# Graph block, last part: the results' stores move from the sync engine's queue to GpSimd's own queue

## The reference

```
x = layernorm(x + attention(x, adj))            # 16 heads, adj added twice as bias
top1   = argmax(mean(x over nodes) @ router_w + router_b)        # one of 4 experts per graph
out    = adj @ (x @ expert_w[top1])
mean, var = moments of out over all graphs of one expert
y      = relu((out - mean) * rsqrt(var + eps) * gamma[top1] + beta[top1])
result = layernorm(x + y)                       # over the 512 features of each node
```

## Time and profile before

| | |
|---|---|
| median of 3 runs | 2736.3 us (2734.73 to 2736.76) |
| the profiled execution's own time | 2736.11 us |
| its span | 2734.3 us |
| last part, from its first DMA issue | from 2483.2 us of the span |
| POOL in the whole span | 885.3 us busy |
| DMA in the whole span | mean 198 GB/s |

### The profile page before, as it was taken

The page is one execution under the profiler, slowest core; times in us unless marked ns, Lnnn a source line. Parts: engine busy times, 40 slices in busy tenths (PEclk is TensorE's granted clock), DMA queues, the critical chain, the costliest instruction groups (busy, mean ns, idle before and its releaser), DMA issues. The chain is left out here.

```text
span 2734.3 us, 61236 instructions
## 1 busy us (share of the span) xinstructions
PE 2580.7 (94%) x20250; PEld 2139.9 (78%) x20250; DVE 2111.7 (77%) x4097; ACT 1783.6 (65%) x6186; POOL 885.3 (32%) x489
## 2 busy tenths in 40 slices
PE   7999999999999999999999999999999999965665
PEld 6788888888888888888888888888888888754554
DVE  5977877877777778778777777777787777864887
ACT  4666666666666666666666666666666666645987
POOL 1132332323323333323223233333232232113776
PEclk9999999999999999999999999999999999988987
DMA  5544544544445445445445444454454454676997
GB/s 215 189 164 179 193 162 172 188 164 175 178 168 189 173 172 190 164 170 193 161 173 189 164 182 168 178 189 164 171 191 164 171 190 158 230 276 259 422 401 304
DMA packets 155055, 540.34 MB, mean 198 GB/s; under 512 B 17586, under 2 KB 50354, under 8 KB 107698
## 3 DMA queue, kind: packets, MB, share of 16 engines
q1 hardware_dynamic: 154802, 536.96, 52.8%
HBM read 427.84 MB, written 109.05 MB: 196 GB/s over the span
## 5 line engine op out<-in xcount | busy, mean ns | idle before, releaser
L667 ACT ACTIVATE prob<-prob,neg_max 128x128 f32<-128x128 f32 x2048 | 792.1, 393 | 6.5 <-DVE abs_max L796 6.5
L426 POOL TENSOR_TENSOR norm<-norm,constants 128x1 f32<-128x1 f32 x128 | 70.2, 549 | 1428.9 <-DVE norm L842 1428.9
L416 POOL TENSOR_TENSOR moments<-moments,conv 128x1024 f32 x128 | 310.4, 2425 | 275.7 <-ACT conv L718 232.9
L667 ACT ACTIVATION_READ_ACCUMULATOR prob<-prob,neg_max 128x1 f32 x2048 | 393.1, 192 | 0.0
L653 ACT ACTIVATE qk<-bank 128x512 f32<-128x512 f32 x256 | 152.9, 598 | 319.8 <-PE bank L435 319.8
L768 DVE SCALAR_TENSOR_TENSOR prob<-bank,adj_in 128x512 f32<-128x512 f32 x512 | 316.9, 682 | 10.5 <-PE bank L435 10.5
L785 DVE TENSOR_TENSOR prob<-prob,inv_sum 128x2048 f32<-128x2048 f32 x128 | 295.6, 2309 | 4.4
L791 DVE TENSOR_REDUCE neg_max<-prob 128x16 f32<-128x2048 f32 x128 | 291.7, 2279 | 0.0
L796 DVE TENSOR_REDUCE abs_max<-prob 128x16 f32<-128x2048 f32 x128 | 291.7, 2279 | 0.0
L660 ACT ACTIVATE probT<-bank 128x512 f32<-128x512 f32 x512 | 265.3, 613 | 25.1 <-PE bank L486 25.1
L402 POOL TENSOR_TENSOR xT_lo<-xT_in,xT_hi 128x1024 fp32r<-128x1024 f32 x62 | 274.7, 4430 | 5.0
(11 more groups left out here) (125 smaller groups left out, 5869.9 us busy)
## 6 DMA issues: line engine op xcount, KB each, us to landing
expert_hi<-expert_hi_scratch SPq DMA_DIRECT2D x124, 1024.0 KB, 4.8
expert_lo<-expert_lo_scratch SPq DMA_DIRECT2D x124, 1024.0 KB, 6.9
x_in<-x SPq DMA_DIRECT2D x128, 256.0 KB, 2.6
x_scratch<-x SPq DMA_DIRECT2D x128, 256.0 KB, 2.5
conv_scratch<-conv SPq DMA_DIRECT2D x128, 256.0 KB, 2.9
conv_in<-conv_scratch SPq DMA_DIRECT2D x32, 1024.0 KB, 12.4
x_in<-x_scratch SPq DMA_DIRECT2D x32, 1024.0 KB, 10.4
out<-x_in SPq DMA_DIRECT2D x32, 1024.0 KB, 11.5
```

Source lines behind the costliest of these rows:

```text
L416: pool.tensor_tensor(acc, acc, conv[:, :, :].rearrange("p k d -> p (k d)"), ALU.add).then_inc(moments_added, 1)
L667: last = act.activation(prob[:, par2, h, :], prob[:, par2, h, :], ACT.Exp, bias=neg_max2[:, par2, h:h + 1], scale=2.0, accum_out=row_sum[: ...
```

## The change

The waits and the DMA of the store leave SP's list and go to a function `store` in POOL's list. POOL calls it behind its own work on a group, for the group two before (`STORE_LAG` = 2). The stores of groups 30 and 31 follow at the end. SP keeps all loads and its wait for each store before the refill.

```
-    REFILL_LAG = 1
+    REFILL_LAG, STORE_LAG = 1, 2
...
             refill_conv(g + 1, (r + 1) % RING, live)
-            if live(g):
-                ends_here = isinstance(g, int) and g == NG - 1
-                sp.wait_ge(pool_finished, (g if ends_here else g + 1) * POOL_TURNS)
-                sp.wait_ge(dve_finished, g + 2 if ends_here else g + 1)
-                sp.wait_ge(act_finished, g + 2 if ends_here else g + 1)
-                sp.dma_start(by_token(out, g * G, G), x1_in[r][:, :]).then_inc(st_g[r], 16)
             h, r1 = g - REFILL_LAG, (r - REFILL_LAG) % RING
...
+        def store(h, r):
+            ends_here = isinstance(h, int) and h == NG - 1
+            pool.wait_ge(pool_finished, (h if ends_here else h + 1) * POOL_TURNS)
+            pool.wait_ge(dve_finished, h + 2 if ends_here else h + 1)
+            pool.wait_ge(act_finished, h + 2 if ends_here else h + 1)
+            pool.dma_start(by_token(out, h * G, G), x1_in[r][:, :]).then_inc(st_g[r], 16)
+
         for r in range(RING):
             group(0, r, lambda g: 0 <= g < NG)
+            if r >= STORE_LAG:
+                store(r - STORE_LAG, r - STORE_LAG)
         with pool.Fori(1, NG // RING - 1, 1) as k:
             for r in range(RING):
                 group(k, r, lambda g: True)
+                store(k * RING + r - STORE_LAG, (r - STORE_LAG) % RING)
         for r in range(RING):
             group(NG // RING - 1, r, lambda g: 0 <= g < NG)
+            store(NG - RING + r - STORE_LAG, (r - STORE_LAG) % RING)
+        for h in range(NG - STORE_LAG, NG):
+            store(h, h % RING)
```

## The result

The changed kernel takes 2744.87 us (median of 8 runs, 2743.44 to 2749.76), the kernel before, run beside it, 2736.61 us (8 runs). The ratio is 1.0032, 95% interval 1.0021 to 1.0042: slower by 8.3 us, 0.3%. The profiled execution took 2745.81 us with a span of 2744.2 us, against 2736.11 and 2734.3 before, 9.9 us of span.

What follows compares the result with a forecast made beforehand. It took ACT's chain as the bound, with DMA full but ahead. Middle and refills cost 0, the tail 6.4 us with the late L1064's 0.6 included: 2736.1 + 6.4 = 2742.5 us, range 2738 to 2756.

Steps and rivals of the forecast that it cites:

- The tail: At the kernel's end, four stores stand where one did: +6.4 us, the later final L1064 included.
- the refills: SP's x1 loads behind the stores, in the last part: issued 10.6 us later, at cost 0.
- the 0.6 of the late L1064: Last group: POOL's issues delay the final L1064, shift and finish by 0.6 us.
- The issue on POOL: Each store issue in POOL's list takes 1.03 us, making POOL's period 6.57 us against 6.20.
- 2.6 us by the last group of a block: POOL falls 0.37 us behind per group, 2.6 us by the end of a block of 8.
- The cover that I computed: Mid-block slack before DVE and ACT feel POOL's delay: 2.2 and 0.8 us, so cost 0 there.
- The first rival, DVE holding the issue up: Each POOL issue waits for one L1172, 1.57 us in all; 2751 to 2756.5 us; 0.16, shared with a slow issue.
- Margins 0.7 and 2.1 us: The last two x1 loads land this long before DVE's joins want them: cost 0, but only just.
- the shift stays: The first refill's 10.6 us delay persists through the last part because the DMA engines are full.
- the signs that the forecast is wrong: POOL rows of 2 us, mid-block L1064 waits, a DVE join behind its load, or an end near the old one.
- the second rival: DMA engines move 3% less with two queues, so DVE and all behind it are 5.0 us late: 2747.5; chance 0.12.
- not slower: ACT's gaps at two loop turns shrink by 3.2 us each, cancelling the tail: 2736 us; chance 0.12.

Runs made afterwards that it cites:

- e4: Changed kernel, but SP issues the last four stores as soon as each group is finished; 2739.8 us.
- e5: Changed kernel with the stores three groups late in place of two; 2751.2 us.
- e2: Changed kernel with lag 0, POOL storing each group directly behind its own work on it; 2738.6 us.
- e7: Changed kernel with a lag of one group and the last four stores issued by SP; 2736.4 us.
- e10: e8 run again unchanged, against new runs of the kernel before; 2731.9 us, ratio 0.9989.
- e3: Kernel before, stores still issued by SP in one queue but each two groups late, refills one group behind the store; 2739.0 us.
- e6: Changed kernel with SP's waits and load order of e3, POOL still issuing the stores two groups late; 2743.6 us.
- e8: e7 with lag 0 in the first eight groups; 2732.2 us.
- e1: Changed kernel with the stores one group late in place of two; 2739.7 us.

## Why the prediction was right or wrong

It said 2742.5 us, slower, for a tail of stores; it became 2744.9, slower. The tail came as forecast; the refills, which were to cost nothing, cost about 3 us, and the sum came close only because they are the smaller part.

**The tail: right, and right in size.** "Four stores, 4.19 MB, stand before the end where one did", 11.1 + 1.3 us, +5.8 us beside the 0.6 of the late L1064. Measured: 10.2 - 4.35 = 5.8 us, and taking it away gave 5.1 back (e4). That it fits to a tenth is partly luck, since its parts were off both ways. Store 28 left 3.5 us ahead of ACT's last end (2730.51 against 2734.01) where I had 2.8, and the four stores had landed 12.1 us after it (2742.6) where I had 12.4: together 1.1 us too much in the forecast. It owed little to the rate that I took, 378 GB/s; that the stretch with it was the "richest in stores" no row of mine showed, and each store more costs 2.5 us, 420 GB/s (e5). Too little by as much was a term that I lacked, POOL's own end: from the last landing to the end of the span it is 1.6 us where it was 0.5. With one store alone at the end, the whole way from the last finish to the end is 6.4 us from POOL (e2) and 4.35 from SP; besides that term, POOL issues 0.5 us later and the store takes 4.2 us to land where it took 3.8. The rows of line 51, the end of the block, show where some of it lies (changed kernel; durations in ns):

```profile
L51 POOLq DRAIN  x1: 9342/9342/9342, 2734.6 to 2734.6; - x1
L51 SPq COMPARE_BRANCH  x1: 38/38/38, 2742.6 to 2742.6; - x1
```

SP has seen all stores land at 2742.6. POOL's drain goes on to 2734.6 + 9.34 = 2743.9, 1.3 us longer, and the block ends with it. In e7, where POOL's own stores are long gone, that drain ends at 2729.8 and costs nothing.

**The issue on POOL: direction right, size too high.** I took 1.03 us from L1064, between 0.33 and 2.08; it is 0.63 in the median:

```profile
L1071 POOL DMA_DIRECT2D out<-x_in x32: 531/633/795, 2528.2 to 2734.6; - x32
```

So POOL's period is 6.22 and not 6.57, and "2.6 us by the last group of a block" is 0.1. The cover that I computed (2.2 + 0.8 us) was not needed. The first rival, DVE holding the issue up, did not happen: all 32 rows of L1071 lie between 0.53 and 0.80 us. The rule of the Trainium skill (SBUF — State Buffer, SBUF: two separate sides) that descriptors wait for a DVE operation in a two-port mode is not borne out by this trace, nor refuted, since no row tells a DVE operation's mode. Six of the 32 issues run beside an L1179: five of them take 0.58 to 0.64 us, no more than the others, and one 0.77.

**The refills: the step that failed.** "Margins 0.7 and 2.1 us: cost 0, but only just. What speaks for the margin is that x1 loads no longer queue behind a store." Two things in it were wrong. The landing of 10.4 us was carried over from a kernel with one queue; it became 22.0. And "the shift stays" at 10.6 us, so that the last two loads could stand for all: SP's first refill of x1 went 12.7 us later than before (2533.84), its last 6.6 us later (2704.3), and what landed latest against before lay in between. The load for group 8 landed 11.3 us later, that for group 17 21.2, that for group 31 11.8. The two that I checked landed at 2717.0 and 2719.5, where I had 2713.8 and 2718.7, and DVE waited for neither. Its eight waits stand before the joins of groups 14, 15, 20 to 23, 28 and 29. A join held up by its load was named among the signs that the forecast is wrong. The chain of the changed kernel shows the last of them:

```profile
2686.45 26.02 DMA x_in<-x_scratch
...
2712.58 0.07 DVE x_in L1168
```

A load issued at 2686.45 lands 26 us later, and DVE starts its join 0.1 us after that. So it was the second rival, "refills come late", with a reason other than mine: not 3% less bandwidth (it was more, 426 against 378 near 2680), but stores that land in 9.4 us beside loads that land in 22, on top of the 20 us at 2510 in which the lag had left the DMA engines nearly idle. ACT's last finish ends 3.5 us later, the 0.55 of the start taken off, where I had 0.6 for the issue and 0 for the refills. In the gross it is more: ACT was ahead of the kernel before by 4.5 us at group 12 (76.8 against 81.2 us behind group 0) and behind by 2.7 at group 28 (2715.76 - 2513.30 against 2712.54 - 2512.75), 7 us lost in between. In e2 and e10, where DVE waits for no load, the lead is 3.4 and 3.0 us at group 12 and 4.4 and 5.3 at group 28, so the loss goes with the late loads. That only 7 of DVE's 15.5 us count is, as I read it, because some of them fall where a turn of ACT's loop left DVE idle anyway; no run shows that apart.

**ACT's gain: half seen.** The rival "not slower" had ACT win 6.4 us from shorter gaps at the turns of its loop. The gaps did not shrink (7.88 and 7.62 us, after 6.64 and 6.97). A gain of 4.5 us came all the same, most of it on entering the loop, where the gap was 1.77 us in place of 3.42 and the ACTIVATEs of group 8 ran without the idle pieces of 0.44 and 0.88 us that they had; the late refills ate it.

**Small slips.** The last six slices before move 230 to 422 GB/s, not 224 to 422, and a finish of DVE at L1172 takes 0.69 us in the median where I took one row's 0.54; nothing hangs on either. The DMA share up to the end is 0.72 from 2730 us on, not 1.

**What the removed part was worth.** SP's 32 issues and waits: nothing that a row shows, as said. SP waits longer now, 175.7 us for stores to land where it was 102.6, and no engine waits for it except through the refills.

Not settled: by what rule the DMA engines share between the two queues (e3 against e6 shows the effect of it, not the mechanism; the Trainium skill, DMA: Bandwidth & Descriptors, Queues, rings and completion order, says that each DMA engine goes round the queues that have work, a packet at a time, with which fast stores and slow loads agree), and why ACT's register loads are shorter with two, and what they are worth. Nor is it known why e6's median lies another 2.9 us above e3's than the ends explain.

## What to carry to other kernels

When a store frees a buffer that a load will fill, moving the store later moves the load later, and where the DMA engines are full the time that they idled at the start is won back slowly: here the loads were 11 us late at the first, 21 at group 17 and still 12 at the last. Look at the loads in the middle too, not at the last ones alone. Count the bytes that the lag pushes towards the end of the kernel, 2.5 us for each MB here. Don't carry a landing time from one queue over to two: splitting them gave the stores a fast way and the loads a slow one. If stores are to leave from another engine, what worked here (for 0.1%) was to keep the lag at what that engine's waits demand, to start with none until the ring is turning, and to issue the last ones from a queue that is empty and whose engine has nothing to drain.

## What the runs showed of the hardware

- A store of 1 MB costs GpSimd 0.53 to 0.80 us to issue (median 0.63), against 0.33 us on SP, and its packets run in a queue of their own kind (q0, software_dynamic).
- In the changed kernel, with loads and stores in two queues, the DMA engines hold 424 to 427 GB/s from 2570 to 2690 us; with all in one queue they fall to 378 to 397 from 2610 us on (kernel before) and to 365 to 389 from 2630 us on (e3). Two queues don't always hold it: e8 moves 384 GB/s from 2570 to 2590 us with the engines full. The kernel does not get faster by it. The Trainium skill (DMA: Bandwidth & Descriptors, Rules for kernel authors) says that spreading DMAs over issuing engines does not help bandwidth; from 2630 to 2670 us, both with full engines, e6 moves 426 and 425 GB/s and e3 389 and 386, so the measurement differs there, for this mix of loads and late stores.
- With the same waits on SP, stores land in 9.4 us and x1 loads in 20.1 in two queues (e6), in 11.4 and 10.4 in one (e3). Over all kernels with two queues the median landing of an x1 load is 12.8 to 24.7 us, and the longest of them do not mark the slowest kernel: e5, the slowest, has 15.1.
- A GpSimd that issued the last store drains 1.3 us beyond its landing (changed, e1, e2, e5).
- ACT's register loads from SBUF between 2600 and 2660 us, with full DMA engines: median 294 to 402 ns beside two queues, 488 and 540 beside one.
